# A graph network on Trainium2: keys of gathered edges made by ScalarE and TensorE instead of VectorE

## The reference

```python
edge_index = jnp.stack([src, dst])                    # dst is sorted
h = jnp.maximum(_layernorm(x, axis=-1), 0.0)
x = x + _L0_gnn_ref(h, edge_index, ...)               # h + segment_sum(h[src], dst); two such convolutions
h = jnp.maximum(_layernorm(x, axis=-1), 0.0)
x = x + _L1_gnn_ref(h, edge_index, ...)               # mlp3(concat(h, segment_sum(mlp3(h[src]), dst)))
```

## Time and profile before

| | before |
|---|---|
| median of 3 runs | 937.06 us (936.87 to 937.08) |
| profiled execution | 940.74 us, span 938.9 us |
| busy in the span: PE, DVE, ACT, POOL | 873.5, 699.8, 480.2, 401.3 us |
| PE's granted clock, mean | 0.987 of full speed |

### The profile page before, as it was taken

The page is one execution under the profiler, slowest core; times in us unless marked ns, Lnnn a source line. Parts: engine busy times, 40 slices in busy tenths (PEclk is TensorE's granted clock), DMA queues, the critical chain, the costliest instruction groups (busy, mean ns, idle before and its releaser), DMA issues.

```text
span 938.9 us, 25210 instructions
## 1 busy us (share of the span) xinstructions
PE 873.5 (93%) x11282; PEld 709.5 (76%) x11282; DVE 699.8 (75%) x656; ACT 480.2 (51%) x573; POOL 401.3 (43%) x281
## 2 busy tenths in 40 slices
PE   0589999999999999899999999999999989999996
PEld 0258888988999999778777677777777867777774
DVE  7789999999999999384555555665545676778773
ACT  2655646554545554364545455445454455554551
POOL 5878888887000000304536656540010144454450
PEclk9969999999999999999999999999999999999998
DMA  3024344344333444315434334443442466788871
GB/s 111 18 87 132 106 154 152 106 135 152 109 123 123 140 140 140 134 34 163 121 114 130 110 116 121 134 125 105 124 119 63 138 200 204 238 233 242 244 215 48
DMA packets 81857, 126.86 MB, mean 135 GB/s; under 512 B 10288, under 2 KB 58544, under 8 KB 81616
## 3 DMA queue, kind: packets, MB, share of 16 engines
q1 hardware_dynamic: 78608, 121.98, 43.1%
q0 software_dynamic: 3136, 3.22, 1.5%
HBM read 84.22 MB, written 40.94 MB: 133 GB/s over the span
## 4 chain that ended last, share of the span: by engine, by line
PE 52%; DVE 4%; ACT 1%; issue 1%; POOL 0%; DVEq 0%; POOLq 0%; ACTq 0%
PE net_ps_hi L1271 15%; PE net_ps_lo L1271 14%; PE net_ps_lo L1288 7%; PE net_ps_hi L1288 7%; PE net_ps_mt L1214 5%; PE net_ps_ft L1214 2%; DVE net_wide L833 1%; PE net_ps_check L1306 1%; DVE hT L926 1%; DVE hT L921 1%; ACT net_wide L1110 1%; DVE net_first L933 1%; PE net_ps_mt L1318 0%; POOL net_wide L879 0%; PE net_ps_mt L1358 0%
## 5 line engine op out<-in xcount | busy, mean ns | idle before, releaser
L1271 PE MATMUL net_ps_hi<-net_wide,net_first 128*128 128x512 f32 (+1 forms) x637 | 248.4, 394 | 1.3 <-POOL net_wide L879 1.3
L1271 PE MATMUL net_ps_lo<-net_wide,net_first 128*128 128x512 f32 (+1 forms) x637 | 240.8, 382 | 0.0
L833 DVE CAST net_wide<-net_raw 128x3584 fp32r<-128x3584 uint8 (+1 forms) x90 | 202.4, 2257 | 42.1 <-PE net_ps_lo L1288 16.3
L1110 ACT ACTIVATE net_wide<-net_raw 128x3584 fp32r<-128x3584 uint8 (+1 forms) x64 | 193.6, 3025 | 78.1 <-PE net_ps_lo L1271 44.9
L338 DVE TENSOR_TENSOR build_hot_lo<-build_grid_lo,build_keys_t 128x4096 bf16<-128x4096 bf16 x100 | 225.1, 2283 | 2.9 <-PE build_ps_cnt L569 2.9
L589 PE MATMUL build_ps_out<-build_parts_pad,build_cnts 128*128 128x195 bf16 x2401 | 223.3, 250 | 2.8 <-ACT build_cnts L456 1.2
L456 ACT ACTIVATE build_cnts<-build_ps_cnt 128x980 uint16<-128x980 f32 (+3 forms) x176 | 151.3, 900 | 128.1 <-PE build_ps_cnt L569 125.6
L589 PEld LDWEIGHTS build_ps_out<-build_parts_pad,build_cnts 128*128 128x128 fp8e4 x2401 | 202.5, 98 | 8.5 <-issue 4.0
L1271 PEld LDWEIGHTS net_ps_hi<-net_wide,net_first 128*128 128x128 f32 x637 | 119.8, 188 | 31.8 <-issue 7.0
L1271 PEld LDWEIGHTS net_ps_lo<-net_wide,net_first 128*128 128x128 f32 x637 | 119.9, 188 | 24.7 <-issue 2.6
L833 POOL CAST net_wide<-net_raw 128x3584 fp32r<-128x3584 uint8 (+1 forms) x28 | 84.8, 3028 | 106.2 <-PE net_ps_hi L1288 52.5
(11 more groups left out here) (171 smaller groups left out, 709.2 us busy)
## 6 DMA issues: line engine op xcount, KB each, us to landing
net_raw<-edge_counts SPq DMA_DIRECT2D x168, 448.0 KB, 3.8
edge_counts<-build_cnts SPq DMA_DIRECT2D x168, 224.0 KB
xres<-in_x SPq DMA_DIRECT2D x1, 1568.0 KB, 7.1
net_raw<-edge_counts SPq DMA_DIRECT2D x14, 112.0 KB, 2.0
out<-xres SPq DMA_DIRECT2D x12, 128.0 KB, 4.2
build_rows<-in_dst_rows,build_row_i POOLq DMA_INDIRECT x49
build_edges<-in_edges,build_start_i POOLq DMA_INDIRECT x49
edge_counts<-build_cnts SPq DMA_DIRECT2D x7, 112.0 KB
```

Of the source, the lines that this page charges most:

```text
L833: return issue(expanded[e % WIDE_RING][:, 0:n, :, :].rearrange("p w a d -> p (w a d)"), raw[e % RAW_RING][:, 0:n, :, :].rearrange("p w a d ...
L1110: expand(act, lambda to, x: nc.scalar.activation(to, x, ACT.Identity), e).then_inc(grown["act"], 1)
L1271: last = nc.tensor.matmul(ps[(b + 1) % 2][:, 0:n * P], first[:, c, lo:lo + H], expanded[e % WIDE_RING][:, 0:n, k, :], start=(c == 0), stop ...
```

## The change

DVE makes no keys any more. For each pair, ACT writes four rows of bf16 numbers into a ring of two (`key_bytes`): the low byte of src divided by 64, the high byte of src times -4, the sign of (low byte - 127.5), and 128 (node - dst). PE adds them up while it turns them: the transposes become four matmuls that accumulate in fp32, with the edge numbers as the stationary operand and an identity (or its negative, over two results of 128 columns) as the moving one. ACT's copy multiplies by 64. The grids are shifted and signed to fit. `turn_keys` waits for one count per pair (`keyed`) instead of one per group. `edges` outlives `build`, and the tally on POOL reads destinations and sources from it.

```diff
@@ constants and grids @@
-                nc.gpsimd.iota(grid_lo[:, :], [[1, P]], 0, 0, **kw).then_inc(consts, 1)
-                nc.gpsimd.iota(grid_a[:, :], [[1, NA]], 0, 0, **kw).then_inc(consts, 1)
-                nc.gpsimd.memset(keys[:, :, NW:2 * NU, :], -1.0).then_inc(consts, 1)
+                nc.gpsimd.iota(node128[:, :], [[P * P, NW]], 0, P, **kw).then_inc(consts, 1)
+                nc.gpsimd.iota(grid_lo[:, :], [[1, P]], 64, 0, **kw).then_inc(consts, 1)
+                nc.gpsimd.iota(grid_a[:, :], [[-P, NA]], 64, 0, **kw).then_inc(consts, 1)
+                nc.gpsimd.memset(cut[:, :], -127.5).then_inc(consts, 1)
@@ vector engine @@
-                def find_keys(g):
-                    lo, hi = SPANS[g]
-                    n = hi - lo
-                    dve.wait_ge(edges_in[g], 16 * n)
-                    src, dst = edges[:, lo:hi, :, 0], edges[:, lo:hi, :, 1]
-                    link(v.tensor_scalar(tile_no[:, 0:n, :], src, 7, None, ALU.logical_shift_right))
-                    v.scalar_tensor_tensor(keys[:, 0, lo:hi, :], tile_no[:, 0:n, :], float(-P), src, ALU.mult, ALU.add)
-                    link(v.scalar_tensor_tensor(scaled[:, 0:n, :], dst, 64.0, tile_no[:, 0:n, :], ALU.mult, ALU.add))
-                    v.tensor_tensor(keys[:, 1, lo:hi, :], scaled[:, 0:n, :],
-                                    node64[:, lo:hi, None].broadcast_to([P, n, RUN]), ALU.subtract).then_inc(keyed, 1)
@@ scalar engine @@
+                def take_bytes(u):
+                    n = both(u)
+                    g = group_of(u)
+                    to = key_bytes[:, u % BYTE_RING, :, 0:n * RUN].rearrange("p k (w e) -> p k w e", e=RUN)
+                    source = edges[:, 2 * u:2 * u + n, :, :].bitcast(U8)
+                    act.wait_ge(edges_in[g], 16 * (SPANS[g][1] - SPANS[g][0]))
+                    nc.scalar.activation(to[:, 0, :, :], source[:, :, :, 0], ACT.Identity, scale=1 / 64)
+                    nc.scalar.activation(to[:, 1, :, :], source[:, :, :, 1], ACT.Identity, scale=-4.0)
+                    nc.scalar.activation(to[:, 2, :, :], source[:, :, :, 0], ACT.Sign, bias=cut[:, 0:1])
+                def take_distances(u):
+                    n = both(u)
+                    to = key_bytes[:, u % BYTE_RING, 3, :].rearrange("p (w e) -> p w e", e=RUN)
+                    for t in range(n):
+                        w = 2 * u + t
+                        last = nc.scalar.activation(to[:, t, :], edges[:, w, :, 1], ACT.Identity, bias=node128[:, w:w + 1],
+                                                    scale=float(-P))
+                    last.then_inc(keyed, 1)
@@ scalar engine, before copy_first_keys(0), then behind copy_first(2, 4) @@
+                take_bytes(0)
+                take_distances(0)
...
                 copy_first(2, 4)
+                take_bytes(1)
+                take_distances(1)
+                take_bytes(2)
+                take_distances(2)
                 round1(2)
@@ scalar engine, loop over pairs u and blocks k @@
                         copy_counts(u, k)
+                        if 0 < u < NU - 2 and k == 0:
+                            take_bytes(u + 2)
+                        if 0 < u < NU - 2 and k == 1:
+                            take_distances(u + 2)
                         for g in range(4, len(SPANS)):
@@ tensor engine @@
                 def turn_keys(u, to):
-                    pe.wait_ge(keyed, group_of(u) + 1)
-                    for k in range(2):
-                        last = nc.tensor.transpose(to[:, k, :], keys[:, k, 2 * u:2 * u + 2, :].rearrange("p w e -> p (w e)"),
-                                                   ident_b[:, :])
-                    return last
+                    pe.wait_ge(keyed, u + 1)
+                    low, tile, top, away = (key_bytes[:, u % BYTE_RING, i, :] for i in range(4))
+                    nc.tensor.matmul(to, top, minus_b[:, None, :].broadcast_to([P, 2, P]), start=True, stop=False)
+                    nc.tensor.matmul(to[:, 0, :], low, ident_b[:, :], start=False, stop=False)
+                    nc.tensor.matmul(to[:, 1, :], tile, ident_b[:, :], start=False, stop=False)
+                    return nc.tensor.matmul(to[:, 1, :], away, ident_b[:, :], start=False, stop=True)
@@ gpsimd, in net @@
-                    nc.gpsimd.tensor_scalar(inside, keys[:, 1, w, :], float(NW), None, ALU.is_lt)
-                    link(nc.gpsimd.tensor_scalar(source, keys[:, 1, w, :], 0.0, None, ALU.is_ge))
-                    link(nc.gpsimd.tensor_tensor(inside, source, inside, ALU.mult))
-                    link(nc.gpsimd.tensor_scalar(source, keys[:, 1, w, :], float(P), None, ALU.mult))
-                    link(nc.gpsimd.tensor_tensor(source, source, keys[:, 0, w, :], ALU.add))
+                    link(nc.gpsimd.tensor_copy(source, edges[:, w, :, 1]))
+                    link(nc.gpsimd.tensor_tensor(source, source, own[:, w, None].broadcast_to([P, PIECE, RUN]), ALU.subtract))
+                    link(nc.gpsimd.tensor_scalar(inside, source, 0.0, None, ALU.is_equal))
+                    link(nc.gpsimd.tensor_copy(source, edges[:, w, :, 0]))
                     link(nc.gpsimd.tensor_tensor(source, source, inside, ALU.mult))
```

45 lines of the change are left out of this document (21 added, 24 removed).

## The result

The changed kernel takes 945.17 us (median of 4 runs, 944.28 to 946.29) beside 937.07 for the kernel before on the same chip: ratio 1.0077, 95% interval 1.0056 to 1.0099. It is slower. The forecast was 945.5 us. The time came out as foretold, but the experiments show that the way there did not: the sum of the prediction holds errors of both signs, and that they nearly cancel is luck. Some executions take longer at a lower granted clock of TensorE (in one experiment, "Rows compared later", four of 12, at 954 us); ratios leave them out.

What follows compares the result with a forecast made beforehand. The prediction took PE to set the pace of the whole steady part. Its terms, 0.4 + 2.35 + 0.64 + 3.7 + 1.4 = +8.5 us, put on the median of 937.06, gave 945.5 us, range 938.5 to 950.

Steps and rivals of the forecast that it cites:

- (a): Start of build: first keys made on ACT instead of DVE, plus a longer PE turn; +0.4 us, bounds 0 and 0.8.
- the prices by columns: ACT's five new instructions a pair, priced by column count: 0.2, 0.2, 0.29 and 2 x 0.24, together 1.17 us.
- (b): Hand-written first part: ten ACT instructions for pairs 1 and 2 queue ahead of the left-over's copy; +2.35 us.
- (c): First part: PE's longer turns for pairs 1 and 2, at the lower clock; +0.64 us, bounds 0.3 and 0.7.
- the prediction's own sign: PE's first third of use comes at about 64.5 us instead of 61.08; the prediction is wrong if it does not move.
- I count it in full: First part: ACT and PE alternate in order, so the ten ACT instructions' whole 2.35 us was charged to the time.
- (d): Steady part, pairs 3 to 24: 22 longer PE turns at 0.17 us each; +3.7 us, bounds 2.2 and 7.0.
- I price it at nothing: Steady part: removing DVE's 12.4 us of key making gains 0, being hidden behind PE's 12.49 us a pair.
- PE sets the pace: From 61 us to the end of build PE, not DVE, limits the kernel; DVE keeps a lead throughout.
- (e): Pairs 3, 7, 9 and 11: PE's turn waits 0.35 us for ACT's distances behind comparisons; +1.4 us, bounds 0 and 3.
- (f): Tally on POOL, five instructions in place of six, reading 16-bit numbers at a step; covered by POOL's idle time, 0.
- The rival that VectorE set the pace: Steady part: PE's slow pairs are waits for hot_lo, so DVE's lost 12.4 us come back; 933.2 us, chance 0.10.

Runs made afterwards that it cites:

- Rows compared later: Changed kernel with ScalarE's comparison of gathered rows, and VectorE's starts, one pair later for group 5 and each later group: 938.3 us, ratio 1.0005.
- before again: The kernel before, with no edit, profiled a second time beside later experiments: 936.45 us.
- after again: The changed kernel, with no further edit, timed and profiled a second time against the kernel before: 945.01 us, ratio 1.0089.

## Why the prediction was right in its number, and wrong in its reading

Counted between the second profiles of the two kernels, which belong to typical runs (936.45 and 943.43 us), the change costs 7.0 us: the net begins at 385.51 in place of 380.85, 4.7 us, and takes 2.3 us more. Against this, step by step:

(a) *The first keys.* ScalarE copies them at 24.69 in place of 24.43 in the first pair of profiles, at 24.84 in place of 24.06 in the second: +0.3 and +0.8 for a predicted +0.4. The new instructions take 0.30, 0.30, 0.39 and 0.34 us: the prices by columns were right.

(b), (c) *The keys of pairs 1 and 2.* The three terms together were +3.4 at the first third of use. In the first pair of profiles it came earlier, 58.25 for 61.08: by the prediction's own sign that was a miss. In the second pair the terms are there, each at its size: TensorE's exchange goes on behind the copy of the left-over at 45.01 in place of 41.89, 3.1 later, which is (a) and 2.3 for the ten instructions; the two turns take 1.06 us (46.19 to 47.25) where they took 0.32. That is 3.9 us late at 47.25, and then it is gone again. Before again, then after again, in TensorE's timeline:

```profile
55.95 5.20 PE L589 MATMUL build_ps_out<-build_parts_pad,build_cnts 128*128 128x195 bf16 x33 [0.97 <-ACT build_cnts L456]
61.08 1.68 PE L569 MATMUL build_ps_cnt<-build_hot_a,build_hot_lo 64*128 64x49 bf16 x120
```

```profile
58.31 2.98 PE L603 MATMUL build_ps_out<-build_parts_pad,build_cnts 128*128 128x195 bf16 x33 [1.24 <-ACT build_cnts L457]
61.23 1.68 PE L583 MATMUL build_ps_cnt<-build_hot_a,build_hot_lo 64*128 64x49 bf16 x120
```

It begins 2.36 us later and ends 0.15 us later. The same 33 matmuls take 5.20 us mostly at the lower level of the clock, 1.2 GHz (granted 0.54 from 56 to 61), and 2.98 at the upper, 2.4 GHz (1.00): what ScalarE cost was given back by a clock that stood higher. In the change's first profile the clock was low there too (4.83 us), so this gain is not a sure one. "I count it in full" held up to 47 us and failed behind it: at the end of the first use, at 61.2, 0.15 us of it was left.

(d) *The turns.* 0.17 us each, exactly; 12.66 between turns. But the sum of 22 of them was set against pairs of 12.49 in the kernel before, which only some have. From the copy of pair 14's keys to that of pair 24's the kernel before took 130.96 us (211.98 to 342.94) and the changed one 126.64 (221.11 to 347.75): 4.3 us less where I forecast 1.7 more. This is the error that mattered: **"I price it at nothing"** for VectorE's 12.4 us, and **"PE sets the pace"** for the whole steady part. In before profiled again the pace is VectorE's in five pairs with a wait, 8.9 us in all; and in seven more, without a wait in the rows, TensorE's turns are 12.61 to 12.75 apart. Five of these are at 12.68, VectorE's own distance there (it begins hot_a at 251.04, 263.73, 276.41 and 289.09). A turn that is longer by 0.17 costs nothing in such a pair. The evidence for the step was a single profile, 3.7 us slower than the median, in which TensorE's gaps had hidden the waits for VectorE. I had noted that the gaps had no named cause, and took them as fixed all the same.

(e) *The wait for the distances.* The place was right, the cause and size were not. I had worked out the comparison's 0.77 us and not asked whether its input is there; the rows were the last thing released, and the wait is 12 to 13.5 us in two places where I had 1.4 in four. The margins that I had looked at were those of the edges.

(f) *The tally* costs nothing, as said. The changed kernel's variant with rows compared later has the new tally too, and its net (380.37 to 934.2) is 553.8 us long, as in before again (380.85 to 934.6). But in the change the net is 2.3 us longer. In 385 to 405 and 745 to 765 us the profile of the change, then of before again:

```profile
385.00:405.00 20.00, 17.61 (x112) 12.96 (x110) 9.29 (x17) 9.39 (x19) 8.47 (x9) 0.83 0.42 138
745.00:765.00 20.00, 18.17 (x85) 13.20 (x85) 16.37 (x26) 10.37 (x13) 6.99 (x3) 0.91 0.66 197
```

```profile
385.00:405.00 20.00, 18.03 (x131) 13.27 (x131) 18.76 (x26) 13.28 (x27) 8.15 (x6) 1.00 0.27 87
...
745.00:765.00 20.00, 17.99 (x79) 12.56 (x77) 14.57 (x23) 13.48 (x14) 8.52 (x3) 1.00 0.64 191
```

The clock dips twice, to 0.83 and 0.91. Neither is tied to the change: the kernel before with ScalarE's work added shows the second (0.91), and the kernel before with the rows compared two steps later the first (0.91). What brings on the dips was not tried.

The terms thus come to: first part about 0; waits in the steady part 13.9 us (13.5 for key bytes, 0.4 for copies) in place of 11.3 (8.9 for VectorE, 2.4 for copies), +2.6; the turns +3.7; together 6.3, where 4.7 was measured up to the net. Of the 1.6 between, some 1.2 are the seven pairs that ran at VectorE's pace (7 x 0.17); the rest is not resolved. The clock does not enter: TensorE starts again below full clock behind long waits in both (0.69 from 193.5 to 199 and 0.68 from 299.6 to 304.9 in before again, 0.78 from 98 to 104 in after again), and by the distances of the turns that costs 3.5 us in either.

So 945.5 us was met by luck. Of the +8.5 us, 3.4 for the first part left some 0.1, 3.7 for the turns are worth some 2.5, and the 1.4 for the wait were 13.5; against this stand 11.3 us of waits that the change took away from the kernel before and for which the sum had no term, and 2.3 us more in the net. The rival that VectorE set the pace had a chance of 0.10 and its mechanism was in the main true; what it lacked was that the freed engine would shut GpSimd out, so that its gain did not show in the time.

## What to carry to other kernels

Before a kernel is read by its waits, compare the profiled execution with the median: gaps put down to issue, without a cause, may belong to that execution alone, and they hide the wait that sets the pace. When work is taken off VectorE, ask who used its pauses; here GpSimd's gathers did, and the rows that ScalarE waits for came 5.5 us later. When work is put into a queue, ask for each wait ahead of it in that queue how much margin its input has, not only how long the work takes: putting the comparison two steps later made a change of +0.9% into one of -0.2%; a whole pair for one group gave -0.3%, which the intervals do not tell apart from it.

## What the runs showed of the hardware that was not expected

- A gather by GpSimd that is issued inside a hot operand of VectorE (bf16 or f16 tensor_tensor) ends 0.81 to 0.93 us after that operand does, in 70 of 70 cases in before profiled again; issued at any other time it takes 0.94 to 1.17 us. So what costs GpSimd time here is less VectorE's busy share than how few pauses and small instructions it has.
- TensorE's small issue gaps come and go between executions of the same program: 7.4 us in 22 before, none in the same kernel profiled again, 21.5 us in 40 in a comparison where the kernel before too was 15 us slower. The Trainium skill (Runtime: NRT & Kernel Launch, section "Instruction fetch mechanics") says that fetching is mostly hidden; by the gaps that agrees with twelve of the fourteen profiles of this study, and would not with two, if fetching is what makes them, which no run here shows.
- The same 33 matmuls of use took 5.20 or 2.98 us, at a granted clock of 0.54 or 1.00, so that a start 2.36 us later cost 0.15 us.
- All of ScalarE's new work (ratio 1.0001) or twice the transposes on TensorE (0.9994) fit into the kernel before at no cost that can be measured. By the rows they fit beside TensorE's waits for VectorE (7.4 and 7.3 us in these two); that this is why was not tried by itself.
